# Expert rows in quadrant-major feature order, loaded in four pieces, and transposed by one block transpose on VectorE instead of four identity matmuls on TensorE

## What is computed

```python
x = x + attention(gate(x, fside, ...), Wq, bq, Wk, bk, Wv, bv, Wo, bo)
x = x + ffn(gate(x, fside, ...), ...)

def ffn(hidden_states, gate_w, w_gate, w_up, w_down, sw_gate, sw_up, sw_down):
    x = hidden_states.reshape(-1, 512)                 # 2048 rows
    scores = sigmoid(x @ gate_w)                       # 32 experts
    # the best 2 of 4 groups, then the best 6 experts of them; weights = scores / their sum
    xs = repeat(x, 6)[argsort(selected)]
    g, u = ragged_dot(xs, w_gate, sizes), ragged_dot(xs, w_up, sizes)   # 512 -> 352
    d = ragged_dot(silu(g) * u, w_down, sizes)                          # 352 -> 512
    expert_out = sum(unsort(d) * weights)
    shared = silu(x @ sw_gate) * (x @ sw_up) @ sw_down
    return expert_out + shared
```

## Time and profile before

| | us |
|---|---|
| median of 3 runs | 2437.08 (2437.06 to 2445.85) |
| span of the profiled execution, first to last instruction | 2410.8 |
| expert loop, first gate product to last | 1413.1 to 2288.8 |

### The profile page before, as it was taken

The page is one execution under the profiler, slowest core; times in us unless marked ns, Lnnn a source line. Parts: engine busy times, 40 slices in busy tenths (PEclk is TensorE's granted clock), DMA queues, the critical chain, the costliest instruction groups (busy, mean ns, idle before and its releaser), DMA issues. The chain is left out here.

```text
span 2410.8 us, 39936 instructions
## 1 busy us (share of the span) xinstructions
PE 2230.7 (93%) x12059; PEld 1925.4 (80%) x12059; DVE 1264.4 (52%) x2102; ACT 1156.9 (48%) x2486; POOL 1440.6 (60%) x965
## 2 busy tenths in 40 slices
PE   2899999999999989898879989999999889999996
PEld 1678888888878878776767869999998779998975
DVE  7868777777755676766754232222222222222276
ACT  4477776777767767676642123333332223332310
POOL 7877777777754557475744035442549986453356
PEclk6899999999999999999989999999999989999998
DMA  4533344543365455555446344443446665444656
GB/s 123 159 102 117 123 127 154 161 127 102 105 227 158 150 163 179 194 183 176 145 166 224 122 142 151 152 140 127 151 151 207 211 192 184 158 144 161 184 184 209
DMA packets 289987, 381.85 MB, mean 158 GB/s; under 512 B 20356, under 2 KB 187336, under 8 KB 285064
## 3 DMA queue, kind: packets, MB, share of 16 engines
q1 hardware_dynamic: 231656, 253.25, 33.4%
q10 hardware_dynamic: 42784, 75.78, 9.4%
q0 software_dynamic: 15360, 50.34, 6.3%
HBM read 265.78 MB, written 121.63 MB: 161 GB/s over the span
## 5 line engine op out<-in xcount | busy, mean ns | idle before, releaser
L1960 POOL TENSOR_SCALAR we_high<-we_raw 128x1408 fp32r<-128x1408 f32 (+1 forms) x95 | 134.1, 1412 | 381.0 <-PE up_e L641 301.0
L1962 POOL TENSOR_TENSOR we_low<-we_raw,we_high 128x1408 fp32r<-128x1408 f32 (+1 forms) x95 | 315.0, 3316 | 7.9
L2148 DVE TENSOR_TENSOR hT_low<-hT_ps,hT_high 128x256 fp32r<-128x256 f32 x127 | 54.0, 426 | 351.5 <-ACT hT_high L2101 351.5
L2161 DVE TENSOR_TENSOR hidden_e<-silu_e,up_e 128x352 f32<-128x352 f32 x127 | 66.2, 521 | 311.9 <-ACT silu_e L2112 311.9
L2112 ACT ACTIVATE silu_e<-gate_e 128x352 f32<-128x352 f32 x127 | 59.0, 464 | 345.3 <-PE up_e L641 345.3
L641 PE MATMUL gate_e<-we_high,xT_high 128*128 x508 | 177.5, 349 | 24.2 <-POOL we_low L1962 21.3
L2117 ACT ACTIVATE rows_out<-down_e 128x512 f32<-128x512 f32 x127 | 75.9, 597 | 216.0 <-PE down_e L641 216.0
L641 PE MATMUL gate_e<-we_high,xT_low 128*128 x508 | 165.7, 326 | 0.0
L641 PE MATMUL gate_e<-we_low,xT_high 128*128 x508 | 165.3, 325 | 0.0
L641 PE MATMUL up_e<-we_high,xT_high 128*128 x508 | 165.1, 325 | 0.0
L641 PE MATMUL up_e<-we_low,xT_high 128*128 x508 | 163.9, 323 | 0.0
(11 more groups left out here) (375 smaller groups left out, 7295.9 us busy)
## 6 DMA issues: line engine op xcount, KB each, us to landing
rows_early<-slots_in ACTq DMA_DIRECT2D x127, 256.0 KB, 3.2
slots_out<-rows_out ACTq DMA_DIRECT2D x127, 256.0 KB, 2.3
we_raw<-L_ffn_w_gate SPq DMA_DIRECT2D x32, 704.0 KB, 5.0
we_raw<-L_ffn_w_up SPq DMA_DIRECT2D x32, 704.0 KB, 4.6
w_ring<-L_attn_Wq SPq DMA_DIRECT2D x64, 256.0 KB, 3.4
q_T<-q_out SPq DMA_DIRECT2D x64, 256.0 KB, 2.5
w_ring<-L_attn_Wk SPq DMA_DIRECT2D x64, 256.0 KB, 3.9
w_ring<-L_attn_Wv SPq DMA_DIRECT2D x64, 256.0 KB, 4.1
```

Of the source, the lines that this page charges most:

```text
L1960: nc.gpsimd.tensor_scalar(wh[:, p, at:to], raw[:, at:to], 1.0, 1.0, ALU.mult, ALU.mult).then_inc(w_hi, 1)
L1962: nc.gpsimd.tensor_tensor(wl[:, p, at:to], raw[:, at:to], wh[:, p, at:to].bitcast(F32), ALU.subtract).then_inc(w_split, 1)
L2161: nc.vector.tensor_tensor(hb[:], sg[:], psu[:], ALU.mult).then_inc(h_done, 1)
```

## The change

A row's 512 features are kept in another order in DRAM: instead of feature = 128 c + 32 j + a (chunk c, quadrant j, place a) they stand as (j, c, a). Then 128 columns of a row hold all that one quadrant of 32 partitions needs.

- The 12 loads of rows (L851) become four DMAs each, one for a chunk c, which put runs of 32 values (128 B) into their places. The wait on POOL counts four times as many. The last batch's copy from PSUM writes in the same order.
- A block of 128 slots is loaded in four DMAs (both at L1652 on SP and at L2083 on ACT), one for a quadrant j: 32 partitions, each with four runs of 512 B (slots b, 32 + b, 64 + b, 96 + b). The loads past the last block are dropped.
- PE's four transposes and its wait for the load go. DVE transposes 32x32 blocks in one instruction, from SBUF to SBUF, at the end of each step, for the block that comes next; it now waits for the load. The result goes into the unused half of `rows_early`.
- ACT's high half and DVE's low half of x read this SBUF tile in place of PSUM.

```diff
+QD = 32
+NQD = P // QD
+def by_quadrant(ap):
+    return ap.rearrange("p (j c a) -> p j c a", j=NQD, a=QD)
+def block_rows(dr, row, j):
+    return dr["xs"][bass.ds(row, P), j * P:(j + 1) * P].rearrange("(i b) f -> b i f", b=QD)
+def quadrant_rows(tile, buf, j):
+    return tile[j * QD:(j + 1) * QD, buf, :].rearrange("b (i f) -> b i f", i=NQD)
...
             def load_rows(u):
-                sp.dma_start(rowt[:].rearrange("p t c -> p (t c)"), dr["x2"][P * u:P * (u + 1), :]).then_inc(rows_in, 16)
+                rows = by_quadrant(rowt[:].rearrange("p t c -> p (t c)"))
+                for c in range(KC):
+                    sp.dma_start(rows[:, :, c, :], dr["x2"][P * u:P * (u + 1), c * P:(c + 1) * P]
+                                 .rearrange("p (j a) -> p j a", a=QD)).then_inc(rows_in, 16)
...
-                    pool.wait_ge(rows_in, 16 * (u + 1))
+                    pool.wait_ge(rows_in, 16 * KC * (u + 1))
...
-                sp.dma_start(f2[:, n, :], dr["xs"][bass.ds(row, P), :]).then_inc(xg_in[n], 16)
+                for j in range(NQD):
+                    sp.dma_start(quadrant_rows(f2, n, j), block_rows(dr, row, j)).then_inc(xg_in[n], 16)
...
-                nc.scalar.activation(rows[:, :, c * P:(c + 1) * P], pst[c % 2][:].rearrange("p (t f) -> p t f", f=P),
-                                     ACT.Copy).then_inc(left, 1)
+                nc.scalar.activation(rows[:].rearrange("p t (j c a) -> p t j c a", j=NQD, a=QD)[:, :, :, c, :],
+                                     pst[c % 2][:].rearrange("p (t j a) -> p t j a", j=NQD, a=QD), ACT.Copy).then_inc(left, 1)
...
-        raw, xg = keep["we_raw"], keep["early"]
+        raw, xg, xt = keep["we_raw"], keep["early"], keep["early"][:, 2:4, :]
...
-                if t := tile(0):
-                    n, p, half = t
-                    pe.wait_ge(x_lo, done(n - 1))
-                    pe.wait_ge(xg_in[p], 16 * half + 16)
-                    for k in range(KC):
-                        last = nc.tensor.transpose(psx[:, k * P:(k + 1) * P], xg[:, p, k * P:(k + 1) * P], ident[:])
-                    last.then_inc(x_T, 1)
...
             def load(n, p):
-                act.dma_start(xg[:, p, :], dr["xs"][bass.ds(row_of(xrow, n, ZERO_ROW), P), :]).then_inc(xg_in[p], 16)
+                row = row_of(xrow, n, ZERO_ROW)
+                for j in range(NQD):
+                    act.dma_start(quadrant_rows(xg, p, j), block_rows(dr, row, j)).then_inc(xg_in[p], 16)
...
-                    nc.scalar.activation(xth[:, p, :, :], psx[:].rearrange("p (k t) -> p k t", k=KC), ACT.Copy).then_inc(x_hi, 1)
-                    load(n + 2, p)
+                    nc.scalar.activation(xth[:, p, :, :], xt[:, p, :].rearrange("p (k t) -> p k t", k=KC), ACT.Copy).then_inc(x_hi, 1)
+                    if n + 2 < NBLK:
+                        load(n + 2, p)
...
+            def transpose_rows(n):
+                p = n % 2
+                dve.wait_ge(xg_in[p], 16 * NQD * (n // 2 + 1))
+                nc.vector.transpose(xt[:, p, :].rearrange("p (k i b) -> p k i b", k=KC, b=QD),
+                                    xg[:, p, :].rearrange("p (i k a) -> p k i a", k=KC, a=QD)).then_inc(x_T, 1)
...
-                    nc.vector.tensor_tensor(xtl[:, p, :, :], psx[:].rearrange("p (k t) -> p k t", k=KC),
+                    nc.vector.tensor_tensor(xtl[:, p, :, :], xt[:, p, :].rearrange("p (k t) -> p k t", k=KC),
                                             xth[:, p, :, :].bitcast(F32), ALU.subtract).then_inc(x_lo, 1)
                 if t := tile(1):
                     n, p = t[:2]
                     dve.wait_ge(s_done, done(n))
                     dve.wait_ge(h_T, done(n - 1))
                     nc.vector.tensor_tensor(hb[:], sg[:], psu[:], ALU.mult).then_inc(h_done, 1)
+                if t := tile(-1):
+                    transpose_rows(t[0])
+            transpose_rows(0)
             step(written_out(0, NBLK))
...
             for n in range(NT):
-                if n < 2:
-                    dve.wait_ge(xg_in[p], 16 * ((NBLK + 3 - p) // 2))
-                else:
+                if n >= 2:
                     dve.wait_ge(o_out[p], 16 * (n // 2))
```

More of the change, by code:

```diff
@@ L2002, in _ @@
         def _(pe):
-            for s in (x_T, gu_mm, h_T, d_mm):
+            for s in (gu_mm, h_T, d_mm):
                 pe.sem_inc(s, CREDIT)
@@ L2131, in _ @@
         def _(dve):
-            for s in (x_lo, h_done, h_lo):
+            for s in (x_T, x_lo, h_done, h_lo):
                 dve.sem_inc(s, CREDIT)
```

## The result

Runs of the changed kernel took 2406.36 us in the median (2402.64 to 2407.7), runs of the kernel before beside them 2437.07; the ratio is 0.9879, 95% interval 0.9856 to 0.9902. That is 30.7 us off; 27.2 were predicted, and the time lies 4 us under the 2410 forecast. The later experiments ran on three chips, on which the kernel before takes 2417 to 2418 us; on two of them the changed kernel ran again and takes 2387 and 2389 us (ratios 0.9871 and 0.9881). So ratios are taken to the kernel before on the same chip.

What follows compares the result with a forecast made beforehand. The prediction took TensorE to bound most expert-loop steps and GpSimd's splits the rest. 44.7 - 13.6 - 0.9 - 3 = 27.2 us off 2437.1 gave about 2410 us, own range 2400 to 2420, 8 in 10 for 2394 to 2430.

Steps and rivals of the forecast that it cites:

- What bounds the kernel: Expert loop: TensorE sets the pace in 104 of 126 steps, GpSimd's weight splits in stretches with one- or two-block experts.
- Part 1: Expert loop: four transposes leave PE, steps go from 6.67 to 6.24 us, 104 x 0.43 = 44.7 us gained.
- part 3: Expert-block loads as four DMAs: landing stays hidden, ACT's three more issues leave 0.8 us before its silu; nothing added.
- Part 2: Block transpose on DVE in the expert loop: takes 0.68 us, hidden up to about 2.5 us; zero cost.
- Part 4: x's low half on DVE, both inputs in SBUF, excludes POOL: 20 x 0.68 = 13.6 us lost, bounds 0 and 27.
- Part 5: Start of the expert loop: transpose, copy and low half in a row delay the first gate 0.9 us, between 0 and 3.
- Part 6: Attention stage's row loads, 12 become 48 with 128 B runs: 3 us lost, from 0 to 21.6.
- The difference of 26.3 us: Runs' median of 2437.08 us lies 26.3 above the profiled span of 2410.8; the prediction kept that difference in its forecast.
- A: Rival: no exclusion costs POOL time, x's low half stays 0.68 us, POOL's pace 14.27; 40.8 off, 2396 us; chance 0.17.
- B: Rival: the transpose excludes POOL too, and some waits reach PE in its own steps; 10.8 off, 2426 us; chance 0.16.
- C: Rival: 128 B runs block SP's queue, weight loads arrive late, PE's projections wait; slower, 2472 us; chance 0.07.
- D: Rival: block pieces land after their 9 us of cover, steps stay at 6.67, only costs remain; 2454 us; chance 0.05.

Runs made afterwards that it cites:

- PSUM version: Changed kernel with DVE's block transpose writing PSUM instead of SBUF, ACT's copy and DVE's low half reading it there: 2386.36 us (0.9864) and 2382.98 us (0.9854).
- the kernel with plain rows: Changed kernel with the attention stage's row loads as one DMA each again, 12 loads of 128 runs of 2 KB: 2389.19 us, ratio 0.9885.

## Why the prediction was right, point by point

**What bounds the kernel**: right. Two regimes, in the same places, and the gain lies wholly in the PE-paced one: the 104 steps lost 38.2 us and the other 22 gained 7.6. Windows of the PSUM version from 1960 to 2140 us still show PE busy 179.3 of 180.

**Part 1** (44.7 us): the mechanism is shown by the kernel with the transposes back, at 6.67 us a step. The term was mis-sized. 6.24 is what a step can do, seen in the one step that has no block behind it; the mean became 6.31. The 104 steps gave 694.1 - 655.9 = 38.2 us, 6.5 less. Some 3.5 us of that belong to part 3, the four loads (steps of 6.31 against 6.28 with one, in one profile). Stretched low halves have at most 1 us in it: without them the same steps take 656.3. The rest, some 0.02 us a step, has no releaser in the trace and stays open.

**Part 2** (0): right. 0.705 us against 0.68 taken, never stretched, with a cover of about 2 us.

**Part 3** (0): that the landing is hidden was right: a piece takes 3.2 to 3.3 us and the last one lands 5.5 us after the first issue in the median, a microsecond later than the 4.5 of the prediction, and DVE waits for it once in the loop. The step that failed is "0.8 us remain" on ACT: it was worked out from issues of 0.35 us, and single ones take up to 1.6 to 2.0. The same line of before had 344 to 702 ns in 127 issues, so four in a row stretch more than one did, which no row of before told; a bound from that line's 702 would have been 2.8 us, and no slack.

**Part 4** (13.6 us): right in mechanism, shown both by taking it away (POOL's pace back to 14.3) and by doubling it (15.8), and too dear: 7.6 us by the 22 steps and 7.8 by the PSUM version, for 13.6. Each collision costs POOL some 0.4 us and not 0.68 (two-block experts 15.1 where 14.27 was, for two low halves), as in the rows at 1865 us: 1.83 against 1.37. Why part of DVE's 0.68 costs POOL nothing isn't shown.

**Part 5** (0.9): from the load of x's rows at the stage's head (L1626 before, L1648 after) to the first gate, the two profiles of before take 165.7 us, the undisturbed ones of after 166.4 and 165.9. Right, at 0.2 to 0.7.

**Part 6** (3): no run resolves it. The means of the marks above lie 3.5 us apart, but single profiles of one kernel differ by as much.

**The sum**: the loop was to fall by 44.7 - 13.6 = 31.1 us and fell by 30.5, because two terms were mis-sized by 6.5 and 6.0 in opposite directions. The agreement to a microsecond is luck; that the terms have these signs and this order isn't.

**The difference of 26.3 us** between span and median was kept for the wrong reason, as a thing around the span. The change doesn't touch it, so nothing came of it. Against the median of other executions a difference holds, not a span.

**The rivals.** A had no exclusion: false, though its ratio, 2396/2437 = 0.983, is near the 0.985 of the PSUM version, in which the exclusion is gone. B had the transpose exclude POOL: false. Its second half, waits that reach PE in its own steps, was true at 1 us at most. C and D did not occur.

## What to carry to other kernels

Before moving work from PE to DVE, look where both inputs of each following DVE operation then lie: an operation that had one input in PSUM and gets both in SBUF waits for GpSimd and holds it up, and here writing the moved result to PSUM gave back nearly 8 us of the loop for one changed tile. Such a wait has a threshold: here one per step was hidden by DVE's gap, and a second in the same step cost 56 us. Read a step's least time as its floor, and take the slack ahead of a queue of DMA issues from the longest issue of the line, not from one.

## What the runs showed of the hardware that I had not expected

A block transpose of 128x512 fp32 on DVE took 705 ns to SBUF, with 17 ns between its shortest and longest of 127 (719 ns to PSUM, 709 to 727), while the subtraction of the same size beside it ranged from 677 to 4266. Two excluded operations in a row don't share one wait: POOL's next operation got in between (1478.53), so the pair took 5.60 us. And 48 loads in runs of 128 B landed in 2.5 us in the median. The Trainium skill, page "DMA: Bandwidth & Descriptors", section "Specifications", speaks of a read-modify-write under 512 B; at 64 KB apiece, next to the 256 KB loads in 2 KB runs that they replaced (3.2 us in the kernel with plain rows), the landing times show no price for it. The packets do show that short runs use the DMA engines worse: among the packets traced from 846 to 1256 us in the second profile of the changed kernel, one of 128 B took 13 ns in the median and one of 512 B 27, which is twice the time for a byte. No run here shows that this cost any time.
